# A DLRM tower with gathered embeddings: rows stored and loaded by parity, first layer's xk turned on TensorE, second tile's gathers held until the first tile is stored

## What is computed

```python
e = jnp.stack([tbl_0[ids[:, 0]], ..., tbl_31[ids[:, 31]]], axis=1)      # (1024, 32, 16)
x0 = xk = e
for W in (W0, W1, W2):                                                  # (32, 32 or 64, 64)
    xk = jax.nn.relu(jnp.einsum('bmd,bhd,mhk->bkd', x0, xk, W))
    outs.append(jnp.sum(xk, axis=2))
h = jnp.concatenate([jnp.concatenate(outs, axis=1), dense_ctx], axis=1) # (1024, 208)
h = jnp.maximum(h @ W_top1 + b_top1, 0.0)                               # 512
h = jnp.maximum(h @ W_top2 + b_top2, 0.0)                               # 256
y = h @ W_top3
```

## Time and profile before

| | us |
|---|---|
| median of 3 runs | 638.65 (638.25 to 639.34) |
| the profiled execution | 643.88 |
| its span, first to last instruction | 642.1 |

### The profile page before, as it was taken

The page is one execution under the profiler, slowest core; times in us unless marked ns, Lnnn a source line. Parts: engine busy times, 40 slices in busy tenths (PEclk is TensorE's granted clock), DMA queues, the critical chain, the costliest instruction groups (busy, mean ns, idle before and its releaser), DMA issues.

```text
span 642.1 us, 8653 instructions
## 1 busy us (share of the span) xinstructions
PE 588.6 (92%) x3084; PEld 216.8 (34%) x3084; DVE 577.6 (90%) x583; ACT 347.7 (54%) x533; POOL 499.6 (78%) x347
## 2 busy tenths in 40 slices
PE   5145789999999999899999999999999999999998
PEld 4143222322243334322343224422343224333444
DVE  4267689999999999799999999999999999999993
ACT  0000545476667567356666467545766567656741
POOL 6705259789999998889888998889888897568770
PEclk9998799999999999899999999999999999999999
DMA  5228998990899404998289937995399818990000
GB/s 127 63 29 214 319 224 197 245 239 4 158 233 243 76 3 55 242 237 181 25 194 229 232 36 139 237 235 104 47 242 235 190 16 191 247 244 5 1 2 0
DMA packets 89149, 95.36 MB, mean 149 GB/s; under 512 B 59501, under 2 KB 68146, under 8 KB 89106
## 3 DMA queue, kind: packets, MB, share of 16 engines
q1 hardware_dynamic: 78318, 90.54, 61.9%
q0 software_dynamic: 6912, 1.78, 3.7%
q10 hardware_dynamic: 3876, 2.49, 1.4%
HBM read 91.37 MB, written 3.94 MB: 148 GB/s over the span
## 4 chain that ended last, share of the span: by engine, by line
PE 24%; DVE 23%; issue 5%; ACT 1%; DVEq 0%
DVE z L1060 22%; PE acc L716 21%; DVE row_sums L1036 1%; PE top L582 1%; ACT xk L784 0%; PE top L573 0%; PE top L570 0%; ACT xk L808 0%; ACT xk L803 0%; DVEq L1058 0%; PE acc L712 0%; PE acc L622 0%; PE xk L610 0%; PE xk L602 0%; PE top L557 0%
## 5 line engine op out<-in xcount | busy, mean ns | idle before, releaser
L1060 DVE TENSOR_TENSOR z<-xk,x0rep 128x1024 f32<-128x1024 f32 x454 | 519.1, 1214 | 21.6 <-DMA x0rep<-x_rows 5.9
L716 PE MATMUL acc<-z,w_sb 128*64 128x512 f32 x1816 | 432.6, 601 | 14.9 <-DVE z L1060 12.4
L546 POOL TENSOR_TENSOR z_pool<-x0rep,xk_copy 128x1024 f32<-128x1024 f32 x122 | 290.4, 2382 | 55.3 <-PE acc L716 27.8
L493 POOL DMA_INDIRECT emb<-tbl,idx x216 | 208.0, 963 | 70.8 <-issue 46.9
L716 PEld LDWEIGHTS acc<-z,w_sb 128*64 128x64 f32 x1816 | 124.1, 137 | 287.7 <-issue 177.9
L808 ACT ACTIVATE xk<-xk_copy 32x1024 f32<-32x1024 f32 x128 | 130.4, 1019 | 94.0 <-DVE z L1060 85.1
L716 PE MATMUL acc<-z_pool,w_sb 128*64 128x512 f32 x488 | 125.6, 593 | 2.6 <-POOL z_pool L546 2.6
L822 ACT ACTIVATE xk_copy<-acc 64x512 f32<-64x512 f32 x128 | 75.4, 589 | 3.3 <-PE acc L716 1.8
L716 PEld LDWEIGHTS acc<-z_pool,w_sb 128*64 128x64 f32 x488 | 34.6, 137 | 70.4 <-issue 63.0
L803 ACT ACTIVATE xk<-lay 128x1024 f32<-128x1024 f32 x15 | 15.4, 1027 | 66.8 <-DVE z L1060 58.5
L654 PE MATMUL acc<-x0rep 125*128 125x160 f32 (+1 forms) x80 | 19.3, 403 | 24.0 <-issue 20.3
(11 more groups left out here) (59 smaller groups left out, 145.1 us busy)
## 6 DMA issues: line engine op xcount, KB each, us to landing
x0rep<-x_rows SPq DMA_DIRECT2D x128, 512.0 KB
lay<-x_rows SPq DMA_DIRECT2D x30, 512.0 KB
emb<-tbl,idx POOLq DMA_INDIRECT x216
squares<-x_rows SPq DMA_DIRECT2D x15, 128.0 KB
x_rows<-emb SPq DMA_DIRECT2D x7, 256.0 KB
x_rows<-emb SPq DMA_DIRECT2D x9, 128.0 KB, 3.6
x0rep<-tbl ACTq DMA_DIRECT2D x8, 78.1 KB
w_wrap<-w ACTq DMA_DIRECT2D x4, 128.0 KB, 7.9
```

Of the source, the lines that this page charges most:

```text
L493: pool.indirect_dma_start(out=emb[:, i % 2, m, :], out_offset=None, in_=tables[m], in_offset=bass.IndirectOffsetOnAxis(ap=idx[:, i, m:m + ...
L546: pool.tensor_mul(z_pool[:, (count - 1) % POOL_RING, :], x0rep[:, g % X0_GROUPS, slot, :], xk_copy[:, side, :]).then_inc(z_pool_ready, 1)
L716: mm = pe.matmul(bank[c * H:(c + 1) * H, :], w[:, tile, :], src[:, c * COLS:(c + 1) * COLS], start=(k == 0), stop=last)
L1060: dve.tensor_mul(z[:, (count - 1) % RING, :], xk[:, bank, :], src).then_inc(z_ready, 1)
```

## The change

- `PICKED` is ordered by parity: three groups of even tables, then three with the odd ones among them. `PICKS` has ten picks, six for tile 0 and four for tile 1, so tile 1 has 18 gathers where it had 12. Tile 0 keeps 12, the six even tables first.
- Tile 0 is saved in two parts (`save_first`). When the even rows are there they are saved, SP waits for that, loads the four even slots of side A and 6 of the 16 pieces of W0; then the same with the odd rows, slots and the plain rows.
- The two layouts of (0, 0, A) no longer come from DRAM: PE turns `emb` by 16 small matmuls for each parity (`turn_rows`), ACT copies the result to `lay` (`copy_rows`), PE selects from that. All of it stands between the picks in PE's order.
- POOL's gathers of tile 1 wait for all four saves of tile 0. `AT_ONCE` is gone, and `IN_PHASE` is changed.
- `LAYER0_FIRST`: the first phase's steps take slots 0, 2, 1, 1. The last three picks of tile 1 are done by DVE between and behind these steps.
- ACT loads 10 pieces of W0 ahead of W1. DVE sums W0 ahead of its picks.
- The first phase's `keep_busy` is gone, and tile 1 loses its own line in `pool_share`: its phases of layer 2 give POOL 3 and 2 steps where it had 4 and 4.

```diff
-LAYER0 = ((0, 0, 0), (1, 0, 1), (2, 1, 2), (3, 1, 1))
+LAYER0_FIRST = ((0, 0, 0), (2, 1, 2), (1, 0, 1), (3, 1, 1))
...
-    if i == 1:
-        return 4
     return {(1, A): 4, (1, Bs): 4, (2, A): 3, (2, Bs): 2}[layer, side]
...
-AT_ONCE = 8
-IN_PHASE = {(0, 1, A): 2, (0, 2, A): 5, (0, 1, Bs): 5, (0, 2, Bs): 6, (1, 1, A): 6,
-            (1, 1, Bs): 6, (1, 2, A): 6, (1, 2, Bs): 6, (2, 1, A): 7, (2, 1, Bs): 7}
+IN_PHASE = {(0, 1, A): 4, (0, 2, A): 6, (0, 1, Bs): 6, (0, 2, Bs): 6, (1, 1, A): 5, (1, 1, Bs): 5}
...
-PICKED = (((1, 4, 7),), ((0, 2), (6, 24)), ((8,), (13, 17)), ((21, 23, 25),), ((27, 29, 31),), ((18, 22, 26, 30),))
-PICKS = [(i, g) for i in range(2) for g in range(len(PICKED))]
+PICKED = (((0, 2), (6, 24)), ((18, 22, 26, 30),), ((4, 8), (1,)), ((7, 17, 27),), ((13, 21, 29),), ((23, 25), (31,)))
+PICKS = [(0, g) for g in range(6)] + [(1, g) for g in range(4)]
...
-            sp.wait_ge(saved_first, 16 * FIRST_SAVES)
-            load_side(0, A)
+            def save_first(odd):
+
+                sp.wait_ge(gathered_first[odd], 16 * len(FIRST_GATHERS[odd]))
+                sp.wait_ge(picked_out, PICKED_EVEN if odd == 0 else len(PICKED))
+                for lo, hi, row in ((0, M, odd), (0, X_ROWS - M, M + odd)):
+                    dst = bass.AP(x0_rows, row * PITCH, [[D, P], [2 * PITCH, (hi - lo) // 2], [1, D]])
+                    sp.dma_start(dst, emb[:, 0, lo + odd:hi:2, :]).then_inc(saved_first, 16)
+                sp.wait_ge(saved_first, 32 * (odd + 1))
+
+            save_first(0)
+            for slot in range(0, SLOTS, 2):
+                load_x0(0, A, slot)
+            load_w0(sp, W0_LOADS, TILES0 * P // M)
+            save_first(1)
+            for slot in range(1, SLOTS, 2):
+                load_x0(0, A, slot)
+                if slot == 1:
+                    load_rows(0, A)
             load_side(0, Bs)
...
             pool.wait_ge(idx_in, 16)
+            pool.wait_ge(saved_first, 16 * FIRST_SAVES)
             for m in GATHERED[1]:
                 gather(1, m, gathered[1])
...
-            for j, m in LATER[None]:
-                gather_later(j, m)
...
+            def turn_rows(odd):
+
+                pe.wait_ge(gathered_first[odd], 16 * len(FIRST_GATHERS[odd]))
+                pe.wait_ge(picked_out, PICKED_EVEN if odd == 0 else len(PICKED))
...
+                for d in range(D):
+                    op = pe.matmul(xk[0:M // 2, 1, d * BLOCKS * ROWS:(d + 1) * BLOCKS * ROWS], emb[:, 0, odd:M:2, d], ident_f[:, 0:BLOCKS * ROWS],
+                                   start=True, stop=True)
+                op.then_inc(rows_turned, 1)
...
+            load_w0(act, 0, W0_LOADS - 2)
+            copy_rows(0)
+            load_w0(act, W0_LOADS - 2, W0_LOADS)
             make_wrap(w1_wrap, w1, w1_wrap_in)
             load_w(w1_sb, w1.tensor, TILES, w1_in, STRAIGHT)
-            act.wait_ge(w0_twice_in, 32)
-            load_w0(act, 0, TILES0 * P // M)
+            copy_rows(1)
```

More of the change, by code:

```diff
@@ L95, in steps_of @@
     if layer == 0:
-        return [("dve", tile, bank, sb) for tile, bank, sb in LAYER0]
+        return [("dve", tile, bank, sb) for tile, bank, sb in (LAYER0_FIRST if (i, side) == (0, A) else LAYER0)]
     share = pool_share(i, layer, side)
@@ L146, in later_gathers @@
     queue = [(j, m) for j in range(2, NT) for m in range(M)]
-    out = {None: queue[:AT_ONCE]}
-    at = AT_ONCE
+    out = {}
+    at = 0
     for i, layer, side in PHASES:
@@ L348, in lays_before @@
         def lays_before(i, side):
-            return sum((j, 0, side) not in SELECTED for j in range(i + 1))
+            return sum((j, 0, side) not in TURNED for j in range(i + 1))
         def copied_before(n):
@@ L670, in select_rows @@
+            def select_rows(layout):
+                pe.wait_ge(rows_copied, layout + 1)
+                if layout == 0:
+                    pe.wait_ge(hot, 6)
                 for c in range(BLOCKS):
                     for half in range(2):
-                        op = pe.matmul(xk[halves[half], layout, c * COLS:(c + 1) * COLS], select[:, layout, halves[half]],
-                                       squares[:, side, c * COLS:(c + 1) * COLS], start=True, stop=True)
+                        op = pe.matmul(xk[halves[half], layout, c * COLS:(c + 1) * COLS], select[:, halves[half]],
+                                       lay[0:M // 2, A, layout, c * COLS:(c + 1) * COLS], start=True, stop=True)
@@ L674, in select_rows @@
                 op.then_inc(xk_ready[layout], 1)
-            pe.wait_ge(w1_in, 16 * 12)
-            pe.wait_ge(constants, 2)
-            pe.wait_ge(hot, len(PICKS))
-            for layout in range(len(E_SHIFT)):
-                select_rows(0, layout)
+            pe.wait_ge(constants, 4)
+            for q in range(4):
+                spread_lines(q)
+            pick(0)
+            spread_lines(4)
+            pick(1)
+            spread_lines(5)
+            pick(2)
+            spread_lines(6)
@@ L682, in _ @@
+            pick(3)
+            turn_rows(0)
+            pick(4)
+            spread_lines(7)
+            select_rows(0)
+            pick(5)
+            spread_lines(8)
+            pick(6)
+            turn_rows(1)
+            pick(7)
+            spread_lines(9)
+            select_rows(1)
+            pick(8)
+            pick(9)
             pe.wait_ge(w0_in, 16 * 16)
@@ L692, in _ @@
                     pe.wait_ge(acc_taken, n - ACCS + 1)
-                elif n:
-                    pe.wait_ge(cleared_out, len(PICKS))
+                else:
+                    pe.wait_ge(cleared_out, max(q + 1 for q in range(len(PICKS)) if ACC_AT[q] == n))
+                if n == 1:
+                    pe.wait_ge(w1_in, 16 * 12)
                 for k, (who, tile, _, _) in enumerate(STEPS[n]):
@@ L708, in _ @@
                     last = k == len(STEPS[n]) - 1
-                    if layer == 0 and k == (2 if n == 0 else len(STEPS[n]) - 1):
+                    if layer == 0 and last:
                         pe.wait_ge(squares_ready, i * SIDES + side + 1)
@@ L718, in _ @@
                     mm.then_inc(step_done, 1)
-                    if n == 0 and k == 0:
-                        keep_busy(1, top)
             make_last()
@@ L1043, in _ @@
                 if n == 1:
+                    pick_rows(between[len(STEPS[0])])
                     dve.wait_ge(step_done, STEP_ENDS[0])
@@ L1051, in _ @@
                     count = DVE_COUNT[n, k]
+                    if n == 0 and k in between:
+                        pick_rows(between[k])
                     if count > RING:
```

164 lines of the change are left out of this document (77 added, 87 removed).

## The result

The changed kernel takes **632.47 us** (median of 4 runs, 630.68 to 633.81) against 638.45 for the kernel before in the same runs: ratio 0.9903, interval 0.9877 to 0.9928. It is faster, as forecast, but by 6.0 us where 23.3 were forecast. Its profiled execution took 633.22 us with a span of 631.4.

A forecast was written before the change was run, and what follows sets the result against it. Settled tiles are bound by DVE, nearly full on PE and POOL, and stay; only the start and tile 3's late x0 can move. -20.8 + 3.4 - 5.9 = -23.3, so 620.6 profiled, 615.3 us median; range 610 to 640.

The forecast's parts named there:

- start: Everything ahead of the settled tiles: POOL's fourth product -20.7 us, DVE's fill for layer 1 -21.0; taken as -20.8 us.
- shares: Tile 1 gives DVE three more multiplies at 1.15 us each, with no idle time to hide them: +3.4 us.
- tile 3: POOL's last gathers come earlier, so DVE's wait for tile 3's x0 goes: -5.9 us, with thin cover of 2 us.
- Step 1: Tile 0's saves: six picks end at 23.4, odd saves land behind the slots at 29.3 + 3.6, all stored at 33 us.
- S: The moment all rows of tile 0 are stored, releasing POOL's tile 1 gathers: forecast 33 us, against 50.45.
- Step 2: Start: POOL's path to its fourth product (-20.7 us) and the ACT, PE and DVE path to layer 1's fill (-21.0) agree.
- Step 3: DVE's 16.72 us wait for the third pick holds the first save until 40.77, POOL's next gather until 50.45, and so layer 0.
- It stands 5.2 above the median: The profiled execution (643.88 us) against the median 638.65: 5.2 taken off the forecast 620.6 to give 615.3 us.
- Rival 1: DVE's long wait for a pick stays and the earlier even slots are given back: +0.3, 639 us; 12%.
- Rival 2: POOL's gathers between odd saves and its first multiply bound the start; slower from S = 56.2 on, 643 us at 60.5; 11%.
- Rival 3: DVE's wait for a pick is only cut short, third pick at about 30, S = 48: -8, 631 us; 12%.
- Rival 4: POOL's 18 gathers each wait for DVE's multiply in progress through the shared port pair: 20.7 us later, 636 us; 3%.

The follow-up runs named there:

- before_again: The kernel before, unchanged, run and profiled once more: 638.98 us, ratio 1.0007.
- after_again: The changed kernel, unchanged, run again as the reference beside the first follow-ups: 632.77 us, ratio 0.9923, span 628.8.
- e1: Changed kernel with PE's select_rows(0) moved from between the fifth and sixth pick to behind the later picks: 630.21 us, ratio 0.9878.
- e2: Changed kernel without POOL's wait for tile 0's saves ahead of tile 1's gathers: 630.42 us (0.9880), in a later set 632.23 us (0.9914).
- e7: Changed kernel with ACT's ctx load four phases later and POOL's wait for tile 0's saves removed: 655.25 us (1.0144), in a later set 631.59 us (0.9907).
- e10: e7 with the top layers' weights loaded behind tile 1's first x0 loads and tile 1's saves behind W2: 626.58 us, ratio 0.9826.
- e9: Kernel before with PE's W1 wait moved to ahead of (0,1,A), one filler matmul pair dropped: 646.97 us (1.0007), in a later set 629.15 us (0.9865).
- e6: Changed kernel with ACT's small ctx load given out four phases later: 636.17 us, ratio 0.9842, in a set where the kernel before took 646.40 us.

## Why the prediction was right or wrong

**The sign, the place and the range were right**: faster, all of it ahead of tile 4, a settled tile unchanged, 632.5 inside 610 to 640. The likeliest value, 615.3, was not: 6.0 us were gained where 23.3 were forecast.

**The term that failed is the start, -20.8.** The table sets the forecast's terms beside DVE's first multiplies in the traces. The start is the time of (1, 2, A), the shares are from there to (2, 1, A), tile 3 from there to (4, 1, A), and the rest is all behind.

| us | forecast |'s execution to the first of after | before_again to after_again |
|---|---|---|---|
| start | -20.8 | 179.82 to 170.89: -8.9 | 175.51 to 169.53: -6.0 |
| shares | +3.4 | +4.7 | +3.4 |
| tile 3 | -5.9 | -7.0 | -7.0 |
| rest | 0 | +0.5 | -1.0 |
| span | -23.3 | -10.7 | -10.6 |

Of the 12.6 us between -23.3 and -10.7 the start has 11.9. The other 4.5 us of the miss come from which executions were profiled (below). Within the start three steps failed.

**Step 1, "S = 33": wrong, 43.85.** It rests on "six by 23.4" and on saves that land at 29.3 + 3.6. In the kernel after the sixth clear came at 35.31. I had ACT's copies and PE's picks as two paths. They are one: the sixth pick stands on PE behind `select_rows(0)`, which stands behind ACT's copy, which stands behind eight DMA issues. But e1 puts the sixth clear at 26.05 and S is still 42.76: the odd saves found the DMA engines full up to 36 us, not up to 29.3. I had costed the four slots as if nothing else used the engines; ACT's W0 and W1 and SP's W0 pieces did. How much each takes was not tried. The even rows were late too: their saves were issued at 20.85 and the slots at 25.10, 3.5 us behind the 21.6.

From S on POOL went as forecast: the 18 gathers took 66.33 - 43.85 = 22.5 us (22.8 forecast), so the 11 us of S arrived whole at the fourth product. PE used it at 80.29, where 70.1 was forecast: 10.5 us ahead of the earlier trace rows instead of 20.7, and 6.2 ahead of the 86.48 of before_again.

**Step 2, "Both paths agree": what stood behind them was left out.** Layer 1 was filled at 53.27 for 51.1, and the odd rows' copy ended at 43.12 for 41.1. But I followed this path to layer 1's fill and took the rest as moving with it. Behind it stood ACT's own issues until 77.28 (e2) and W2's landing at 89 us (e7, e10), which had cover before. e2 shows the size: with POOL's first product at 58.00 the time was 630.42 us in one set and 632.23 in another. In before_again PE reached (0, 2, A) at 93.8, and W2 lands at 89.1 in after_again: PE's start of that phase could give 4.7 us until W2 moved.

**Step 3, "This stall holds ... layer 0": true of the execution that I read, but its end frees next to nothing.** Without the stall the loads of x0 come early, fill the DMA engines, and W1 lands at 56.48, where the stall had let it land by 42. PE's first selection then starts 0.2 us earlier and DVE's first multiply 3.4 us, not 16.7. What started layer 0 at 41.56 in the kernel after is that its wait for W1 stands a phase later; e9 shows this wait by itself: -8.6 us.

**"It stands 5.2 above the median": counted twice.** The profiled execution had the stall, and in the set in which the stall turned up all 17 runs stood above 643. I forecast that the stall goes and still took the 5.2 off the rest. After's own profiled execution stands 0.75 above its median. These are the other 4.5 of the 17 us missed.

**ACT and PE.** Turning at nothing held for the even rows, which PE had turned before ACT came. For the odd ones ACT stood waiting until 42.11, the last 2.83 us for those matmuls, near the bound of 2.4. Not in the forecast was TensorE's granted clock: 0.50, the lower of its two levels (1.2 and 2.4 GHz), from 28 to 40 us in the kernel after, where PE had worked for 0.41 us between 23.81 and 29.70. The eight matmuls of a selection took 3.67 us there, and 1.93 us at 43.26.

**Shares, +3.4, and tile 3, -5.9: right.** For the shares before_again and after_again give 3.39. In them DVE waited 3.8 us and 0.5 us for x0 in the stretch of the earlier trace rows, and before_again 3.0 us more behind it. From (2, 1, A) to (4, 1, A):

```profile
213.49:361.69 148.20, 142.13 (x744) 49.19 (x740) 141.24 (x132) 87.20 (x134) 131.23 (x96) 0.98 0.67 146
```

```profile
210.90:352.06 141.16, 139.13 (x738) 47.57 (x736) 140.68 (x131) 87.12 (x134) 124.80 (x92) 1.00 0.70 165
```

The end of these two executions is 10.6 us apart and the medians of their runs 6.2. The first stands 2.2 us above its median and the second 2.2 below, so the two fit, but a term of a us or two is not told from two executions.

**The rivals.** Rival 1 had no stall to keep. Rival 2's mechanism happened in part: the odd saves behind the loads were served late and PE stood at the first `z_pool` step (5.30 us), but S stayed short of the 56.2 from which it would have made the kernel slower. Rival 3's 631 us is near the measured time by another cause; that is luck. Rival 4 did not happen: gathers beside DVE's multiplies took 0.94 and 0.95 us, 1.25 apart. The rule of the Trainium skill (SBUF — State Buffer, "SBUF: two separate sides") is tied to DVE's two-port modes; I had applied it to these multiplies without showing that they run in one, and this trace shows no wait by it.

**Open.** Why the wait for a pick comes in some sets of runs and not in others, and whether after itself is free of it there. If it is, as e6 suggests, the change is worth some 1.6% in such a set rather than 0.9%.

## What to carry to other kernels

Before pricing a wait at its length, ask for each engine which semaphore it would stand at next, and when that one would be set once the wait is gone. That need not be when it is set now: here the loads that the wait had held back made W1 at least 14 us later. Follow a shortened path until it meets every load that had cover before (here ctx, W2, late POOL products), since each of them is paid one after the other. And where one profiled execution is above the median, look whether the thing that the change removes is what puts it there, and get a second trace before building on a wait that only one has.
